# Attention heads on one core: scratch writes of GpSimd halved and partly left out, and a gather moved between two scatters

## The chip, the cores and the metric

One core of one Trainium2 chip. The metric is the device time of one execution in microseconds (us); the median of three runs of the kernel before is 1216.95 us (1214.2 to 1217.95).

## The reference, cut to what matters

A transformer layer: modulated layer norm, attention, then a mixture of experts. The change touches the attention alone. For each of 32 (batch, head) pairs the 409 queries of largest norm out of 2048 are picked; only they attend, and their results are put back at their places, zeros elsewhere.

```python
query_norms = jnp.linalg.norm(Q, axis=2)
_, top_idx = jax.lax.top_k(query_norms, top_u)          # 2048 // 5 = 409
Q_sel = jnp.take_along_axis(Q, top_idx[:, :, None], axis=1)
attn = jax.nn.softmax(jnp.einsum('bud,bld->bul', Q_sel, K) * scale, axis=-1)
out_sel = jnp.einsum('bul,bld->bud', attn, V)
out_full = out_full.at[jnp.arange(BH)[:, None], top_idx].set(out_sel)
```

## The kernel before, in words

The program is a row of blocks with a barrier between them: set-up, projection of Q, K and V, selection of the 409 queries, attention (`attend_block`, line 803, some 223 to 643 us), routing, experts. Only `attend_block` is touched.

It works through N = 32 heads in a software pipeline. Each head's 409 queries are three full chunks of 128 rows (FULL = 3) and a tail of 25 rows; the tails of four heads (GH = 4) share one tile, `qtail`. The engines' parts for head n:

- **TensorE** (`run`, line 1160): 16 score tiles of head n (`scores_tile`, line 1113, index j), and between them the 13 score chunks of the heads n + 1 and n + 2 (`scores_chunk`, lines 1097 and 1100), the transposes of the queries of head n + 3 (`turn_q`, lines 1068 and 1072, at j = 8, once per head), the products with V (line 1123), the folding of the result (line 1132) and the transposes of the row maxima (`turn_max`, line 1139, at j = 13). `turn_q` waits for the three gathers of its head and for the gather of the tails of its group of four.
- **VectorE** (line 961): one maximum over each of the 13 chunks (`maximum`, line 966), each raising the semaphore `a_done`; after a head's last one `minus_maximum` (lines 973 to 979): three small copies, a reduction, a cast to bfloat16 (line 978) and a subtraction, for which `turn_max` waits; and `finish` (lines 987 to 990) for the head before, which needs the scatters of two heads back to be over.
- **ScalarE** (line 1021): the exponentials (line 1036) and copies out of PSUM.
- **SyncE** (line 873): three loads of K per head.
- **GpSimd** (line 884): the irregular transfers. In its loop over n (line 937) it issues the three gathers of the queries of head n + 4 (`gather_chunk`, line 887), copies V of head n + 3 into its tile (`spread_v`, line 903), waits for `out_done`, and issues the three scatters of the results of head n - 1 (`scatter_chunk`, line 906). Every fourth head a gather of the tails of the next four heads (`gather_tails`, line 898) and a scatter of four heads' tails (`scatter_tails`, line 920) come after the three scatters.

What sets GpSimd's order is `turn(n, at)` (line 911), ahead of each of these transfers, seven times per head, also where no transfer follows. It writes a scratch tile `idle` of 128x512 float32 that nobody reads, waits for that write to end, and then waits until VectorE has done so many maxima: the thresholds are `13 (n + 1) + TURNS[at]` with TURNS = (7, 9, 11, 13, 15, 17, 19). So the three gathers wait for the maxima 7, 9 and 11 of head n + 1, the first scatter for its 13th and last, the next ones for the 2nd and the 4th of head n + 2, and the transfers of tails for the 6th.

Of the kernel before, what the change touches and what calls it, by code (L numbers as in the profile page):

```python
# [8 lines left out]

# [1 line left out]

# [3 lines left out]
F32 = mybir.dt.float32  # L17
# [8 lines left out]
P = 128  # L26
# [22 lines left out]
GH, GN = 4, N // 4  # L49
# [17 lines left out]
def wait(eng, sem, value):  # L67

    if isinstance(value, int) and value <= 0:
        return  # L70
    eng.wait_ge(sem, value)


def places(nc, own, block):

    sems = []

    def clear():
        nc.clear_and_free_semaphores(sems)
        nc.all_engine_barrier()  # L80

    def sem(name):
        sems.append(nc.alloc_semaphore(f"{block}_{name}"))
        return sems[-1]

    own.callback(clear)
    return (lambda name, shape, dt: own.enter_context(nc.sbuf_tensor(f"{block}_{name}", shape, dt)),
            lambda name, shape, dt: own.enter_context(nc.psum_tensor(f"{block}_{name}", shape, dt)),
            sem)
# [713 lines left out]
def attend_block(nc, ctx, io, cst):  # L803

    with ExitStack() as own:
        sb, ps, sem = places(nc, own, "attend")
        CH = 512
        NK = L // CH
        FULL = QT - 1
# [17 lines left out]
        recip = sb("recip", [P, QT], F32)  # L827
        outs, otail = cst["outs"], cst["otail"]
        fold = sb("fold", [P, HD + 1], F32)
        idle, idled = sb("idle", [P, 512], F32), sem("idled")  # L830
        p_a = [ps(f"p_a{i}", [P, 512], F32) for i in range(3)]
        p_b = [ps(f"p_b{i}", [P, 512], F32) for i in range(3)]
        p_o = ps("p_o", [P, 512], F32)
# [33 lines left out]
        def has(n):  # L867

            return not isinstance(n, int) or 0 <= n < N

        with nc.Block() as block:

            @block.sync
            def _(sp):
                def load_k(n, u):

                    wait(sp, b_ps, TPB * (n - U + 1))
                    rows = io["k3_d"][bass.ds(n, 1)].rearrange("a r d l -> (a r d) l")
                    for at, count in STACK_K:
                        sp.dma_start(kt[u][at * HD:(at + count) * HD, :], rows[0:count * HD, :]).then_inc(k_here[u], 16)  # L880

                steps(sp, load_k)

            @block.gpsimd
            def _(pool):
                def gather_chunk(n, c):
                    pool.indirect_dma_start(out=qsel[n % U][:, c, :], out_offset=None, in_=io["q3_d"],  # L887
                                            in_offset=bass.IndirectOffsetOnAxis(ap=cst["idx"][:, n, c:c + 1], axis=0)).then_inc(q_here[n % U], 16)

                def gather(n):  # L890
                    wait(pool, q_ps, n - U + 1)
                    for c in range(FULL):
                        gather_chunk(n, c)

                def gather_tails(g):

                    wait(pool, q_ps, GH * g)
                    pool.indirect_dma_start(out=qtail[:, :], out_offset=None, in_=io["q3_d"],
                                            in_offset=bass.IndirectOffsetOnAxis(ap=cst["tidx"][:, g:g + 1], axis=0)).then_inc(tail_here, 16)

                def spread_v(n):
                    wait(pool, pv_ps, GRP * (n - U + 1))
                    pool.tensor_copy(vh[n % U][:, :, 0:HD], vn[:, :, n, :]).then_inc(vh_done, 1)

                def scatter_chunk(n, c):
                    pool.indirect_dma_start(out=io["attn_d"], out_offset=bass.IndirectOffsetOnAxis(ap=cst["idx"][:, n, c:c + 1], axis=0),  # L906
                                            in_=outs[n % 2][:, c, :], in_offset=None).then_inc(scattered[n % 2], 16)

                TURNS = (7, 9, 11, 13, 15, 17, 19)

                def turn(n, at):

                    pool.memset(idle[:, :], 0.0).then_inc(idled, 1)  # L913
                    pool.wait_ge(idled, len(TURNS) * n + at + 1)
                    wait(pool, a_done, min(NA * (n + 1) + TURNS[at], NA * N))

                def scatter_tails(g):

                    pool.wait_ge(out_done, GH * (g + 1))
                    pool.indirect_dma_start(out=io["attn_d"], out_offset=bass.IndirectOffsetOnAxis(ap=cst["tidx"][:, g:g + 1], axis=0),  # L920
                                            in_=otail[:, g, :], in_offset=None).then_inc(tail_out, 16)

                gather_tails(0)
                for n in range(3):
                    gather(n)
                step = Chain(pool, g_step)
                step(pool.memset(fold[:, :], 0.0))
                for g in range(GRP):
                    last = pool.affine_select(out=fold[:, :], in_=fold[:, :], compare_op=ALU.not_equal, fill=1.0,
                                              base=-32 * g, pattern=[[-1, HD + 1]], channel_multiplier=1)  # L930
                    if g < GRP - 1:
                        step(last)
                last.then_inc(fold_done, 1)
                for n in range(3):
                    spread_v(n)
                gather(3)
                for n in range(N):
                    if has(n + 4):
                        pool.wait_ge(q_ps, n + 1)
                    for c in range(FULL):  # L940
                        turn(n, c)
                        if has(n + 4):
                            gather_chunk(n + 4, c)
                    if has(n + 3):
                        spread_v(n + 3)
                    if has(n - 1):
                        pool.wait_ge(out_done, n)
                    for c in range(FULL):
                        turn(n, FULL + c)
                        if has(n - 1):  # L950
                            scatter_chunk(n - 1, c)
                    turn(n, 2 * FULL)
                    if n % GH == 1 and n > 1:
                        scatter_tails(n // GH - 1)
                    if n % GH == 0 and n // GH + 1 < GN:
                        gather_tails(n // GH + 1)
                for u in range(2):
                    pool.wait_ge(scattered[u], 16 * FULL * (N // 2 - u))
                pool.wait_ge(tail_out, 16 * (GN - 1))
# [1015 lines left out]
```

## Time and profile before

| | |
|---|---|
| median of three runs | 1216.95 us |
| the profiled execution, its own time | 1216.12 us |
| its span in the trace | 1214.3 us |
| TensorE busy | 999.9 us, 82% of the span |
| VectorE busy | 906.4 us, 75% |
| ScalarE busy | 649.6 us, 53% |
| GpSimd busy | 740.3 us, 61% |
| GpSimd's scratch writes (line 913) | 224, 120.3 us |
| mean granted clock of TensorE | 0.90 of full speed |

The span is the trace's first to last instruction; the execution's own time has 1.8 us around it. Shares are means over all blocks: in the attention block alone they are others. An interval between two rows of the same line in neighbouring heads is the time that one head takes.

### The profile page before, as it was taken

Reading aid. Unit: us, or ns where it says so; the run is one execution under the profiler, and the core shown is the slowest. Engines: PE = TensorE matmul, PEld = TensorE weight load, DVE = VectorE, ACT = ScalarE, POOL = GpSimd, SP = SyncE. Lnnn points to the kernel's source line nnn. Section 1 sums busy time; section 2 is a strip of 40 time slices with the busy share of each in tenths; the row PEclk is TensorE's granted clock in tenths of the full one; section 3 lists DMA queues with packets and bytes.
Section 4 is the critical chain, followed back from the end, with each engine's and each line's share of the span. In section 5 each row is a group of like instructions: output and inputs, shape, how many; then the busy total and the mean of one; then the engine's idle time right before and its main releaser. Section 6 shows DMA issues by size and latency. Waiting matters only on the chain. (4 is left out here: it accounts for less than half of the span.)

```text
span 1214.3 us, 29465 instructions
## 1 busy us (share of the span) xinstructions
PE 999.9 (82%) x7725; PEld 613.1 (50%) x7726; DVE 906.4 (75%) x2189; ACT 649.6 (53%) x1448; POOL 740.3 (61%) x873
## 2 busy tenths in 40 slices
PE   7999101399999998999995774189999999999995
PEld 4444001133333332333334663167778888888894
DVE  3885689788887786887844887857778777777774
ACT  2777196067776775776773542344544444444441
POOL 1687382458888878888867884025445445544543
PEclk9999555579999998999997986589999999999998
DMA  6244772201111111111105993099893233222332
GB/s 225 104 143 162 242 234 67 59 18 47 35 46 32 45 33 32 46 45 33 32 4 182 268 280 103 5 251 226 218 222 62 47 50 52 43 47 48 52 44 27
DMA packets 129166, 118.71 MB, mean 98 GB/s; under 512 B 18064, under 2 KB 117072, under 8 KB 129104
## 3 DMA queue, kind: packets, MB, share of 16 engines
q1 hardware_dynamic: 106840, 95.02, 26.8%
q0 software_dynamic: 20480, 21.53, 11.1%
q10 hardware_dynamic: 1784, 1.44, 0.4%
q8 instruction: 26, 0.43, 0.2%
q14 instruction: 36, 0.29, 0.1%
HBM read 57.27 MB, written 37.60 MB: 78 GB/s over the span
## 5 line engine op out<-in xcount | busy, mean ns | idle before, releaser
L966 DVE TENSOR_REDUCE attend_mxh<-attend_p_a 128x1 f32<-128x512 f32 x416 | 265.2, 686 | 67.9 <-PE attend_p_a L1097 46.3
L1036 ACT ACTIVATE w<-attend_p_b 128x409 f32<-128x409 f32 x480 | 229.0, 514 | 107.8 <-PE attend_p_b L1113 90.0
L1730 POOL DMA_INDIRECT out_x<-expert_ys,expert_drop x72 | 122.0, 1695 | 193.2 <-DVE expert_ys L1872 138.5
L1837 ACT ACTIVATE expert_hr<-expert_p,b1t 128x256 f32<-128x256 f32 (+1 forms) x376 | 134.3, 424 | 195.6 <-PE expert_p L1775 132.2
L1113 PE MATMUL attend_p_b<-attend_qt,w 98*128 98x409 bf16 x480 | 165.7, 349 | 0.3 <-ACT w L1036 0.3
L1097 PE MATMUL attend_p_a<-w,attend_qt 96*128 96x512 bf16 x384 | 152.8, 401 | 3.3 <-ACT attend_qt L1027 1.9
L1797 PE MATMUL expert_p<-w,expert_hhi 128*128 x800 | 136.7, 273 | 0.6 <-DVE expert_ys L1872 0.2
L1775 PE MATMUL expert_p<-expert_xhi,w 128*128 128x256 f16 x800 | 136.4, 273 | 0.0
L913 POOL MEMSET attend_idle<- 128x512 f32 x224 | 120.3, 537 | 8.4 <-DVE otail L990 4.6
L1720 POOL DMA_INDIRECT expert_xs<-h_d,expert_take x72 | 74.0, 1027 | 74.7 <-DVE expert_take L1876 53.6
L1123 PE MATMUL attend_p_o<-w,attend_vh 128*32 128x409 f32 x1024 | 118.1, 534 | 1.1 <-ACT w L1036 0.6
L887 POOL DMA_INDIRECT attend_qsel<-q_d,idx x96 | 92.8, 966 | 38.2 <-POOL attend_idle L913 19.1
L906 POOL DMA_INDIRECT attn_d<-outs,idx x93 | 91.6, 985 | 30.7 <-DVE attend_mxh L966 16.1
L1797 PE MATMUL expert_p<-w,expert_hlo 128*128 x400 | 109.0, 273 | 0.0
L1113 PEld LDWEIGHTS attend_p_b<-attend_qt,w 98*128 98x128 bf16 x480 | 46.6, 98 | 115.7 <-ACT w L1036 78.2
L1897 DVE TENSOR_TENSOR expert_hlo<-expert_hr,expert_hhi 128x512 f16<-128x512 f32 x144 | 100.5, 698 | 5.0
L1895 DVE CAST expert_hhi<-expert_hr 128x512 f16<-128x512 f32 x144 | 62.8, 436 | 48.4 <-ACT expert_hr L1837 41.2
L1797 PEld LDWEIGHTS expert_p<-w,expert_hhi 128*128 128x128 f16 x800 | 78.2, 98 | 13.2 <-issue 3.7
L1775 PEld LDWEIGHTS expert_p<-expert_xhi,w 128*128 x800 | 78.3, 98 | 9.2
L1775 PE MATMUL expert_p<-expert_xlo,w 128*128 128x256 f16 x400 | 76.4, 273 | 0.0
L1775 PE MATMUL expert_p<-expert_xhi,expert_wu 128*128 128x128 f16 x704 | 67.2, 221 | 1.7 <-DVE expert_xlo L1880 1.4
L1792 PE MATMUL expert_p<-w,expert_hhi 128*128 x176 | 60.9, 380 | 5.3 <-DVE expert_ys L1872 2.8
(353 smaller groups left out, 1994.8 us busy)
## 6 DMA issues: line engine op xcount, KB each, us to landing
expert_wu<-w SPq DMA_DIRECT2D x88, 256.0 KB
q_d<-project_q SPq DMA_DIRECT2D x32, 256.0 KB
w<-in_L_ffn_w SPq DMA_DIRECT2D x16, 512.0 KB, 4.2
route_wraw<-in_L_ffn_w SPq DMA_DIRECT2D x16, 512.0 KB, 5.2
w<-k_d SPq DMA_DIRECT2D x32, 192.0 KB
k_d<-project_k SPq DMA_DIRECT2D x45, 128.0 KB
x<-in_L_attn_x SPq DMA_DIRECT2D x8, 512.0 KB, 8.8
attn_d<-zero SPq DMA_DIRECT2D x8, 512.0 KB
```

Of the source, the lines that this page charges most:

```text
L887: pool.indirect_dma_start(out=qsel[n % U][:, c, :], out_offset=None, in_=io["q3_d"], in_offset=bass.IndirectOffsetOnAxis(ap=cst["idx"][:, ...
L913: pool.memset(idle[:, :], 0.0).then_inc(idled, 1)
L966: dve.tensor_reduce(mxh[:, c, k:k + 1], chunk_bank(a)[:, :], AX, ALU.max).then_inc(a_done, 1)
L1036: act.activation(prob[:, j, :], tile_bank(j)[:, 0:TOP], ACT.Exp, scale=SCALE).then_inc(prob_done, 1)
L1097: last = pe.matmul(into[:, :], qt[u][0:KR, c * P:(c + 1) * P], kt[u][0:KR, k * CH:(k + 1) * CH], start=True, stop=True)
L1113: pe.matmul(tile_bank(j)[:, 0:TOP], kt[u][0:KR + 2, j * P:(j + 1) * P], qt[u][0:KR + 2, 0:TOP], start=True, stop=True).then_inc(b_ps, 1)
L1123: last = pe.matmul(p_o[32 * w:32 * w + VC, 0:TOP], vh[u][:, j, :], prob[:, j, :], start=(g == 0), stop=(g == TPB // GRP - 1), tile_positio ...
L1730: pool.indirect_dma_start(out=out, out_offset=bass.IndirectOffsetOnAxis(ap=drop[u][:, s:s + 1], axis=0), in_=ys[u][:, s, :], in_offset=Non ...
L1775: last = pe.matmul(p_1[g][:, f, rows], w, xp[u][:, k, rows], start=(n == 0), stop=(n == 3 * KD - 1))
L1797: last = pe.matmul(p_2[s][:, 0:D], hp[u][:, f, s * P:(s + 1) * P], w(slice(part, part + 1)), start=(f == 0 and n == 0), stop=(f == FB - 1 ...
L1837: last = act.activation(hr[g % 2][:, f, rows], p_1[g][:, f, rows], ACT.Relu, bias=cst["b1t"][:, bass.ds(e[s] * FB + 2 * g + f, 1)], scale= ...
L1897: dve.tensor_tensor(hlo[u][:, 2 * g:2 * g + 2, :], hr[g % 2][:, :, :], hhi[u][:, 2 * g:2 * g + 2, :], ALU.subtract).then_inc(hlo_done, 1)
```

## The change

GpSimd's part of `attend_block` alone. There are two scratch tiles of 128x256 elements in place of one of 128x512, used in turns, each with a semaphore of its own: a write waits for the write before the last one, and nothing waits for the write just issued. Ahead of the first scatter, behind the copy of V, nothing is written. Turns without a transfer behind them are left out. The gather of four heads' tails stands between the first and the second scatter (threshold 15), and in those heads the second and the third scatter wait for the thresholds 17 and 19.

```diff
-        idle, idled = sb("idle", [P, 512], F32), sem("idled")
+        idle, idled = [sb(f"idle{i}", [P, 256], F32) for i in range(2)], [sem(f"idled{i}") for i in range(2)]
...
+                rows = itertools.count()
+
+                def space():
+
+                    i = next(rows)
+                    wait(pool, idled[i % 2], i // 2)
+                    pool.memset(idle[i % 2][:, :], 0.0).then_inc(idled[i % 2], 1)
+
                 def turn(n, at):
 
-                    pool.memset(idle[:, :], 0.0).then_inc(idled, 1)
-                    pool.wait_ge(idled, len(TURNS) * n + at + 1)
+                    if at != FULL:
+                        space()
                     wait(pool, a_done, min(NA * (n + 1) + TURNS[at], NA * N))
...
                 for n in range(N):
                     if has(n + 4):
                         pool.wait_ge(q_ps, n + 1)
-                    for c in range(FULL):
-                        turn(n, c)
-                        if has(n + 4):
+                        for c in range(FULL):
+                            turn(n, c)
                             gather_chunk(n + 4, c)
                     if has(n + 3):
                         spread_v(n + 3)
+                    fresh = n % GH == 0 and n // GH + 1 < GN
+                    if fresh and not has(n - 1):
+                        turn(n, FULL + 1)
+                        gather_tails(n // GH + 1)
                     if has(n - 1):
                         pool.wait_ge(out_done, n)
-                    for c in range(FULL):
-                        turn(n, FULL + c)
-                        if has(n - 1):
+                        for c in range(FULL):
+                            turn(n, FULL + c + (fresh and c > 0))
                             scatter_chunk(n - 1, c)
-                    turn(n, 2 * FULL)
+                            if fresh and c == 0:
+                                turn(n, FULL + 1)
+                                gather_tails(n // GH + 1)
                     if n % GH == 1 and n > 1:
+                        turn(n, 2 * FULL)
                         scatter_tails(n // GH - 1)
-                    if n % GH == 0 and n // GH + 1 < GN:
-                        gather_tails(n // GH + 1)
```

## Rows read from the trace of the kernel before

**Rows 1.** Window: us; busy us (count) of PE, PEld, DVE, ACT, POOL; PE clock, DMA share, GB/s.

```profile
255.80:598.70 342.90, 335.75 (x2468) 120.69 (x2470) 277.71 (x614) 242.83 (x532) 287.19 (x402) 0.98 0.16 39
```

**Rows 2.** Timeline of TensorE, line 1068, once per head: start us, us, engine, line, operation.

```profile
255.76 0.35 PE L1068 MATMUL attend_p_a<-identb,attend_qsel 128*32 128x128 bf16 x9
...
267.39 0.35 PE L1068 MATMUL attend_p_a<-identb,attend_qsel 128*32 128x128 bf16 x9
...
302.44 0.35 PE L1068 MATMUL attend_p_a<-identb,attend_qsel 128*32 128x128 bf16 x9
...
314.58 0.35 PE L1068 MATMUL attend_p_a<-identb,attend_qsel 128*32 128x128 bf16 x9
...
448.76 0.35 PE L1068 MATMUL attend_p_a<-identb,attend_qsel 128*32 128x128 bf16 x9
...
463.56 0.51 PE L1068 MATMUL attend_p_a<-identb,attend_qsel 128*32 128x128 bf16 x9 [3.09 <-DMA attend_qtail<-q_d,tidx]
...
478.08 0.35 PE L1068 MATMUL attend_p_a<-identb,attend_qsel 128*32 128x128 bf16 x9
...
598.66 0.35 PE L1068 MATMUL attend_p_a<-identb,attend_qsel 128*32 128x128 bf16 x9
```

**Rows 3.** Waits, 242 to 640 us: who waits for whom, us in total, times, longest.

```profile
PE attend_p_a L1068 <- DMA attend_qtail<-q_d,tidx: 6.9, 4, 3.1
```

**Rows 4.** Timeline of GpSimd: one head and the next head's first gather.

```profile
337.68 1.00 POOL L887 DMA_INDIRECT attend_qsel<-q_d,idx  x1 [0.28 <-POOL attend_idle L913]
338.67 0.54 POOL L913 MEMSET attend_idle<- 128x512 f32 x1
...
343.38 1.02 POOL L906 DMA_INDIRECT attn_d<-outs,idx  x1 [0.28 <-DVE attend_mxh L966]
...
349.38 1.00 POOL L887 DMA_INDIRECT attend_qsel<-q_d,idx  x1 [0.28 <-POOL attend_idle L913]
```

**Rows 5.** Timeline of GpSimd where a gather of last rows comes between.

```profile
461.12 1.00 POOL L898 DMA_INDIRECT attend_qtail<-q_d,tidx  x1 [0.28 <-POOL attend_idle L913]
...
462.93 0.97 POOL L887 DMA_INDIRECT attend_qsel<-q_d,idx  x1 [0.27 <-POOL attend_idle L913]
```

**Rows 6.** Groups of GpSimd: count, busy us, mean ns of one, idle before it.

```profile
L913 POOL MEMSET attend_idle<- 128x512 f32 x224 | 120.3, 537 | 8.4 <-DVE otail L990 4.6 <-DVE attend_mxh L966 2.1
L887 POOL DMA_INDIRECT attend_qsel<-q_d,idx x96 | 92.8, 966 | 38.2 <-POOL attend_idle L913 19.1 <-DVE attend_mxh L966 13.2 <-issue 5.9
L906 POOL DMA_INDIRECT attn_d<-outs,idx x93 | 91.6, 985 | 30.7 <-DVE attend_mxh L966 16.1 <-POOL attend_idle L913 13.3 <-DMA attn_d<-outs,idx 1.4
...
L903 POOL COPY attend_vh<-v 128x256 f32<-128x256 f32 x32 | 12.8, 404 | 0.3
...
L1367 POOL MEMSET keepf<- 128x256 f32 x1 | 0.3, 318 | 0.0
```

**Rows 7.** Timeline of all engines around the cast of line 978, GpSimd late.

```profile
304.39 0.41 POOL L903 COPY attend_vh<-v 128x256 f32<-128x256 f32 x1
304.42 0.87 DVE L978 CAST attend_mpart<-attend_mneg 128x4 bf16<-128x4 f32 x1
...
304.73 0.53 POOL L913 MEMSET attend_idle<- 128x512 f32 x1
```

**Rows 8.** The same around a later cast, GpSimd on time.

```profile
599.21 0.69 DVE L966 TENSOR_REDUCE attend_mxh<-attend_p_a 128x1 f32<-128x512 f32 x1
...
600.63 0.17 DVE L978 CAST attend_mpart<-attend_mneg 128x4 bf16<-128x4 f32 x1
600.68 0.99 POOL L906 DMA_INDIRECT attn_d<-outs,idx  x1 [0.92 <-DVE attend_mxh L966]
```

**Rows 9.** The same around a cast that began under a gather's last 0.07 us.

```profile
426.22 0.97 POOL L887 DMA_INDIRECT attend_qsel<-q_d,idx  x1 [0.27 <-POOL attend_idle L913]
...
427.12 0.64 DVE L978 CAST attend_mpart<-attend_mneg 128x4 bf16<-128x4 f32 x1
427.18 0.55 POOL L913 MEMSET attend_idle<- 128x512 f32 x1
```

More of the change, by code:

```diff
@@ L12 @@
+import itertools
 from contextlib import ExitStack
```

## The prediction

> **What bounds the kernel now.** I read the attention block by stage first, then one row per head on TensorE, then who waits for whom, then GpSimd instruction by instruction. The window [rows 1] holds 28 heads: TensorE is busy in 335.75 of 342.90 us, GpSimd in 287.19. By busy share TensorE is the bound, and GpSimd has room. The other views correct that.
>
> TensorE turns each head's queries once, at a fixed place, so the distance between two such rows is the time of a head [rows 2]. Undisturbed it is 267.39 - 255.76 = 11.63 us, and that head has no gap on TensorE. The mean is (598.66 - 255.76) / 28 = 12.25 us. So 342.90 - 28 x 11.63 = 17.3 us are lost. A large part is lost at one kind of place: the turn of every fourth head, which waits for the gather of four heads' last rows (four such waits, 6.9 us [rows 3]). The worst is at 463.56, after 3.09 us of idleness. The two intervals around it last 14.80 and 14.52 us, 6.06 over twice 11.63: the matmul row itself is longer behind the idle stretch (0.51 against 0.35 us), which is the lower of the two clock levels, 1.2 instead of 2.4 GHz. The pattern comes four times in the 28 heads, and its eight intervals together have 14.8 us of the 17.3.
>
> Why that gather is late stands in GpSimd's timeline [rows 4]. From one head's first gather to the next one's pass 349.38 - 337.68 = 11.70 us without a pause that it chooses: a transfer of about 0.97, a write of 0.54, 0.27 to 0.28 until the next transfer. That is already over TensorE's 11.63. With a transfer of last rows it is 1.27 us more: 462.93 - 461.12 = 1.81 for transfer, write and gap [rows 5], less the 0.54 of a write that every head has there with nothing behind it. Per four heads, two of them with such a transfer, 4 x 11.70 + 2 x 1.27 = 49.3 us against TensorE's 46.5. **GpSimd is the bound**, though a quarter of its queue is scratch writes: 224 x 537 ns = 120.3 us [rows 6].
>
> The other 2.5 us of the 17.3 have another place. The cast of line 978 takes 0.17 us on its own [rows 8] and up to 0.87 where GpSimd works: begun at 304.42, 0.03 us behind GpSimd's copy, it ends at 305.29, 0.03 after the write that follows the copy [rows 7]. The transposes of the maxima wait for it. In that head the interval is 314.58 - 302.44 = 12.14, 0.51 over, so TensorE forgives about 0.87 - 0.51 = 0.36 us of cast.
>
> **The change, part by part.** The durations come from one execution, 1216.12 us with a span of 1214.3; the median of the runs is 0.8 above it.
>
> (a) Shorter scratch write. The nearest row is a GpSimd write of 128x256 float32 at 318 ns [rows 6], against 537.
>
> (b) Fewer of them. Three per head ahead of gathers in 28 heads, 84; two ahead of scatters in 31 heads, 62; seven ahead of each kind of last rows, 14: 160 for 224. The one ahead of the first scatter goes, and so does the empty turn in each head.
>
> (c) No wait for one's own write. What stands between a write and a transfer then? At best nothing (the gap passes under the write), at worst the time that a transfer needs when its semaphore comes late: the maximum that began at 599.21 ends at 599.90, the scatter it releases starts at 600.68, 0.78 us later [rows 8]. The write would then lie inside the 0.78. I take today's gap of 0.27, since most thresholds are long reached.
>
> GpSimd's sum for a plain head: 3 gathers x 0.966 + 3 scatters x 0.985 + copy 0.404 = 6.26 [rows 6]; 5 writes x 0.318 = 1.59; 6 gaps x 0.27 = 1.62; together 9.47 us. With last rows, 1.00 + 0.318 + 0.27 = 1.59 more: 11.06. Both are below 11.63, so GpSimd waits for VectorE at its thresholds instead of running behind, and cannot carry lateness into the next head.
>
> (d) The gather of last rows moves ahead of two scatters. It waits for the 2nd maximum instead of the 6th. Being issued on time, it ends some 4.2 us behind a head's last maximum: 0.73 to the cast [rows 8], 0.17 for it, about as much for the subtraction behind it, two maxima of 0.69, then 0.78 and 1.00. It lands 463.56 - 462.12 = 1.44 us later [rows 2, 5]. TensorE's row of line 1068 comes 599.90 - 598.66 = 1.24 us ahead of that maximum, so it wants the data 11.63 - 1.24 = 10.4 us behind it, over 4 us after they are there. Queued behind it are two scatters, delayed by at most 1.59 us; their reader is the result tile of two heads later, so that costs nothing while the cover of a whole head lasts. SyncE's queue is not passed. By these numbers the move matters little once (a) to (c) hold; were GpSimd late, it would bring the gather forward by two turns, about 3.1 us, as much as the longest wait.
>
> (e) The cast. With GpSimd on time it starts at 600.63 and the first scatter at 600.68: it keeps its 0.17 us. The pattern of rows 8 comes three times, at the last three casts, each time with the scatter 0.05 to 0.06 us behind the cast. That is inside the 0.36 that TensorE forgives. But whichever starts first goes first: in rows 7 and 9 GpSimd's work was there already or followed without a gap, and the cast waited; a timely scatter could do the same (rival 1).
>
> TensorE is late next, with every one of its 11.63 us filled; its granted clock is 0.98 of 2.4 GHz in the mean of the 28 heads with the four waits among them [rows 1], so I expect no new cost there. Sum: -14.8 - 2.5 = -17.3 us. In the block's end GpSimd's last scatter comes up to 1.8 us earlier, but VectorE's last result does not; I count 0 and keep -1.8 as an end of the range. 1216.12 - 17.3 = 1198.8 for the profiled execution, 1199.6 for the median.
>
> On this the Trainium skill, SBUF — State Buffer, Who interferes with whom, says that a VectorE copy or cast in its two-port mode and a GpSimd operation exclude each other, whichever starts first holding the ports to its end. The trace agrees (0.87 against 0.17). By that rule alone a scatter that wins the race costs a head what rival 1 says, and one that loses it costs nothing; which of the two it will be, the page cannot say.
>
> **The rivals.**
> 1. **The scatter beats the cast**, slower than before. The margin is 0.05 us (600.68 against 600.63). Nothing is written ahead of that scatter now; if that lets it start more than 0.05 earlier, the cast waits for it and for the write that follows without a gap. A cast that began 0.07 before a gather's end waited through the next write too, 0.64 [rows 9]. Price: 0.985 + 0.318 = 1.30 us of cast, less 0.36: 0.94 per head, 12.57 x 28 = 352.0, 9.1 over today's 342.9: 1226. Against it: the wait ahead of the scatter is the same semaphore after the same maximum. Chance 0.08.
> 2. **It beats it in half the heads.** 0.47 us per head, 13.2 of the 17.3 given back: 1213. Or with the cast held for the scatter alone, in some heads: around 1208. Chance 0.12.
> 3. **The gap is 0.78, not 0.27.** With the write inside it, a plain head takes 5.86 + 0.40 + 6 x 0.78 = 10.9 us and one with last rows 10.9 + 1.78 = 12.7; mean 11.8, over 11.63 again by 0.2: up to 28 x 0.2 = 5.6 given back: 1203 to 1205. Chance 0.07.
> 4. **Nothing changes**, because something else holds TensorE at 12.25. For it only the busy share of 98%; against it the undisturbed 11.63. 1217. Chance 0.05.
>
> **The numbers.** The forecast has 0.68 (1197.5 to 1202). The likeliest time is 1199.5. The range 1196 to 1211 takes in rival 3 and most of rival 2 and leaves out rivals 1 and 4, 0.13, and a part of 2. A measurement of this kernel can tell about 0.3%, 3.7 us, from no change. Faster by more than that: forecast, rival 3 and three quarters of rival 2, 0.84. Within it: the rest of 2 and rival 4, 0.08. Slower: rival 1, 0.08.
>
> **What would show it.** 160 writes near 318 ns; TensorE's row of line 1068 every 11.63 us, also at every fourth head, and no wait for the gather of last rows; GpSimd's idle time put down to VectorE's maxima, with a 0.78 us start after each; the cast at 0.17 in all heads. Wrong if casts of about 1 us appear, if GpSimd still goes from transfer to write to transfer without waits, or if intervals stay at 11.7 and more with GpSimd on time.

## The result, and the profile after

The changed kernel takes 1231.58 us (median of 4 runs, 1227.55 to 1236.65) against 1216.69 for the kernel before (4 runs): ratio 1.0139, interval 1.0112 to 1.0165. I had forecast 1199.5 and said "slower" with a chance of 0.08. The profiled execution took 1227.55 us with a span of 1225.7.

GpSimd's own part came nearly as computed. Its groups in the changed kernel (line, operation, names, count, then busy us, mean ns of one, idle before it and who ended it), to be held against [rows 6]:

```profile
L888 POOL DMA_INDIRECT attend_qsel<-q_d,idx x96 | 93.1, 970 | 59.8 <-DVE attend_mxh L978 49.9 <-issue 9.9
L907 POOL DMA_INDIRECT attn_d<-outs,idx x93 | 91.6, 984 | 87.8 <-DVE attend_mxh L978 76.9 <-issue 6.7 <-DVE otail L1002 3.8
...
L918 POOL MEMSET attend_idle<- 128x256 f32 x160 | 52.7, 329 | 0.2
```

160 writes of 329 ns take 52.7 us where 224 took 120.3, and the transfers now wait for VectorE's maxima instead of for GpSimd's own writes: GpSimd is on time. The groups of VectorE show the cast of line 990 at 173 ns in the mean, and no slow one among the 32:

```profile
L978 DVE TENSOR_REDUCE attend_mxh<-attend_p_a 128x1 f32<-128x512 f32 x416 | 267.3, 686 | 86.7 <-PE attend_p_a L1109 71.9 <-issue 9.3 <-PE attend_p_a L1112 0.2
...
L990 DVE CAST attend_mpart<-attend_mneg 128x4 bf16<-128x4 f32 x32 | 5.5, 173 | 1.1
```

No wait of TensorE for the four heads' last rows is left, where [rows 3] had 6.9 us. Undisturbed heads take 11.63 us, as forecast. But the window of the 28 heads is longer than before, not shorter (columns as in [rows 1]):

```profile
255.71:611.71 356.00, 343.64 (x2466) 121.01 (x2466) 272.12 (x614) 243.10 (x532) 231.56 (x352) 0.95 0.16 38
```

356.00 us, 13.1 over the 342.90 of [rows 1]. TensorE is busy in 343.64 of them, 7.9 more than before with the same matmuls, and idle in 12.4. Where the first loss comes from is to be seen in the timeline of all engines in the head whose turn is at 303.52, where the moved gather has just been issued and its two scatters follow (start us, us, engine, line, operation; weight loads and some rows left out):

```profile
309.05 1.00 POOL L907 DMA_INDIRECT attn_d<-outs,idx  x1 [0.17 <-issue]
...
310.04 0.34 POOL L918 MEMSET attend_idle<- 128x256 f32 x1
...
310.06 0.38 PE L1109 MATMUL attend_p_a<-w,attend_qt 96*128 96x512 bf16 x1
...
310.28 0.34 PE L1125 MATMUL attend_p_b<-attend_qt,w 98*128 98x409 bf16 x1
...
310.54 0.98 POOL L907 DMA_INDIRECT attn_d<-outs,idx  x1 [0.17 <-issue]
310.71 0.52 ACT L1048 ACTIVATE w<-attend_p_b 128x409 f32<-128x409 f32 x1
...
311.22 1.46 DVE L978 TENSOR_REDUCE attend_mxh<-attend_p_a 128x1 f32<-128x512 f32 x2 [1.54 <-PE attend_p_a L1109]
311.52 0.33 POOL L918 MEMSET attend_idle<- 128x256 f32 x1
...
311.95 0.91 ACT L1048 ACTIVATE w<-attend_p_b 128x409 f32<-128x409 f32 x2 [0.72 <-PE attend_p_b L1125]
```

TensorE's chunk of line 1109 that began at 310.06 ends at 310.44. VectorE, idle since 309.68, begins its maximum only at 311.22, 0.78 us later. The tile of line 1125 that began at 310.28 ends at 310.62; ScalarE is free at 311.23 and begins its exponential at 311.95. Both engines stand still though by these rows their input is computed. **What is late is the word that it is there**: the trace also has the times of the signals themselves (a signal is the update of a semaphore by which TensorE tells its reader), and it has a signal 0.02 to 0.1 us ahead of the reader's start in 17 of the 18 stops counted below, 0.5 to 1.7 us behind the end of the matmul's row, where the median over all tiles is 0.014. GpSimd meanwhile goes through a scatter, a write, a scatter and a write, begun 310.54 - 309.05 = 1.49 us apart. Eighteen such stops of ScalarE, of 0.5 to 1.8 us, lie in the 28 heads and add up to some 19 us (a stop is counted from 0.4 us between the later of the matmul's end and ScalarE's own, and the start of the exponential).

What follows a stop costs as much again. The windows of the head with that stop and of the next two (the third column from the end is the granted clock as a share of 2.4 GHz):

```profile
303.52:315.53 12.01, 11.81 (x89) 4.25 (x88) 8.97 (x22) 7.74 (x18) 9.12 (x15) 1.00 0.18 42
315.53:330.33 14.80, 13.35 (x89) 4.52 (x89) 10.57 (x24) 9.63 (x21) 9.53 (x15) 0.88 0.15 34
330.33:343.43 13.10, 13.10 (x89) 4.40 (x88) 9.88 (x24) 8.74 (x20) 7.74 (x13) 0.87 0.15 37
```

12.01, 14.80 and 13.10 us. In the second, TensorE is idle for 1.45 us and the granted clock falls to its lower level, 1.2 GHz, for a part of the head; the same 88 or 89 rows take 13.35 and 13.10 us of its time instead of 11.63. So the loss goes into idle time first and then into slower matmuls: of the 356.00 - 325.64 = 30.4 us over 28 heads of 11.63, 12.4 are idle time of TensorE and 18.0 are rows that take longer.

### The profile page after: what moved, and what is told of

Same layout as the page of the kernel before. It is cut to its first block and busy times, and to the rows that moved or that the text cites. A ratio compares the mean times of both kernels' runs of the same rounds, so it can differ in the third digit from the quotient of the medians.

```text
span 1225.7 us, 29249 instructions
## 1 busy us (share of the span) xinstructions
PE 1007.7 (82%) x7725; PEld 611.1 (50%) x7726; DVE 899.9 (73%) x2189; ACT 649.4 (53%) x1448; POOL 679.0 (55%) x809
## 3 DMA queue, kind: packets, MB, share of 16 engines
q10 hardware_dynamic: 1784, 1.44, 0.4%
## 5 line engine op out<-in xcount | busy, mean ns | idle before, releaser
L1125 PE MATMUL attend_p_b<-attend_qt,w 98*128 98x409 bf16 x480 | 168.6, 355 | 0.7 <-issue 0.5
L1135 PE MATMUL attend_p_o<-w,attend_vh 128*32 128x409 f32 x1024 | 122.7, 553 | 2.1 <-ACT w L1048 1.0
L553 PE MATMUL project_p_qv<-wtb,project_ht 128*128 128x512 f32 x128 | 60.0, 593 | 0.0
```

The lines of the kernel that those rows point to most:

```text
L1125: pe.matmul(tile_bank(j)[:, 0:TOP], kt[u][0:KR + 2, j * P:(j + 1) * P], qt[u][0:KR + 2, 0:TOP], start=True, stop=True).then_inc(b_ps, 1)
L1135: last = pe.matmul(p_o[32 * w:32 * w + VC, 0:TOP], vh[u][:, j, :], prob[:, j, :], start=(g == 0), stop=(g == TPB // GRP - 1), tile_positio ...
```

## Experiments

I started from the theory that GpSimd's transfers now follow one another too closely, with three rivals: that the missing wait for the own write does it by itself, that the moved gather does it, and that a GpSimd on time is in the way wherever it is. The first group of four had one ingredient taken out in each.

**e1_own_wait**, in `space()` of the changed kernel:

```diff
                     pool.memset(idle[i % 2][:, :], 0.0).then_inc(idled[i % 2], 1)
+                    pool.wait_ge(idled[i % 2], i // 2 + 1)
```

> The changed kernel, but every scratch write of 256 is waited for before the next transfer, as in the kernel before. In the changed kernel 19 or so stalls stand out, in which ScalarE and VectorE both sit idle though their inputs are there; each falls on the third (or fourth) GpSimd transfer in a row whose starts are 1.44 to 1.50 us apart. Crowding theory (what counts is the distance of the starts): the distance grows to 0.97 + 0.32 + 0.27 = 1.56 to 1.60 us; if the limit lies below that the time falls to about 1200 us, if above it, it stays within 8 us of the changed kernel's 1231. Own-wait theory (a write in flight under the preparation of the next transfer does the harm, the distance does not matter): the stalls vanish, 1198 to 1203 us.

Measured: 1196.08 us (4 runs), ratio 0.9839 (0.9807 to 0.9872). The 28 heads take 327.3 us, and 27 of them 11.63 to 11.69.

**e2_rows512**, the changed kernel with longer scratch rows:

```diff
-        idle, idled = [sb(f"idle{i}", [P, 256], F32) for i in range(2)], ...
+        idle, idled = [sb(f"idle{i}", [P, 512], F32) for i in range(2)], ...
```

> The changed kernel with the two scratch rows at 512 elements again, still in turns and without a wait for the own write. Crowding theory: the starts are 0.97 + 0.54 + 0.16 = 1.67 us apart, so fewer and shorter stalls or none, 1200 to 1215 us. Own-wait theory: the write is still in flight when the next transfer is prepared, so the stalls stay, 1225 to 1235 us.

Measured: 1194.92 us, 0.984 (0.9808 to 0.9873).

**e3_tails_back**, the changed kernel with the last rows gathered behind the scatters again:

```diff
-                            turn(n, FULL + c + (fresh and c > 0))
+                            turn(n, FULL + c)
                             scatter_chunk(n - 1, c)
-                            if fresh and c == 0:
-                                turn(n, FULL + 1)
-                                gather_tails(n // GH + 1)
...
+                    if fresh:
+                        turn(n, 2 * FULL)
+                        gather_tails(n // GH + 1)
```

> The changed kernel with the gather of four heads' last rows back behind the three scatters. Theory that the move alone does the harm (it makes rows of three and four close transfers out of pairs in seven heads): 1200 to 1210 us. Crowding theory in general: the last rows' transfer then stands before the next head's gathers and closes up with them, so the rows of three move but most of them stay: 1220 to 1232 us. Own-wait theory: no difference from the changed kernel, 1226 to 1236 us.

Measured: 1195.15 us, 0.9828 (0.979 to 0.9866), with 98 transfers begun under 1.52 us behind the one ahead of them, and no stop. No theory of mine had this time.

**e4_lean512**, the kernel before with its 512-element write and its wait, without the empty turns and without the write ahead of the first scatter:

```diff
-                    for c in range(FULL):
-                        turn(n, c)
-                        if has(n + 4):
+                        for c in range(FULL):
+                            turn(n, c)
                             gather_chunk(n + 4, c)
...
-                    turn(n, 2 * FULL)
...
+                    if at != FULL:
+                        pool.memset(idle[:, :], 0.0).then_inc(idled, 1)
```

> The kernel before with its one scratch row of 512 and its own wait, but without the empty turns and without the write ahead of the first scatter; the gather of last rows stays behind the scatters. GpSimd's sum is 3 x 0.966 + 3 x 0.985 + 0.404 + 5 x 0.537 + 6 x 0.27 = 10.6 us per plain head and 12.3 with last rows, mean 11.45, just below TensorE's 11.63. Crowding theory: starts stay 1.78 us or more apart and nothing stalls, so the heads run at 11.63 to 11.75 us: 1199 to 1206 us. If the timeliness of GpSimd itself is what hurts (its transfers on time collide with something), it is slow like the changed kernel, 1220 us or more.

Measured: 1199.71 us, 0.9866 (0.983 to 0.9902), 28 heads in 329.4 us.

Each ingredient alone seemed able to cure it, and e3 contradicted the crowding theory: the same pace as in the changed kernel, and nothing stopped. I read that as an interplay of all three, and looked for the place. That was a mistake: the group held no run of the changed kernel itself. The second group, on another occasion, tried the place.

**e5_wait_fresh** and **e6_wait_rest**: the wait of e1 only at the three writes ahead of the moved gather and the two scatters behind it (21 writes), and only at the other 139.

```diff
+                    if own:
+                        pool.wait_ge(idled[i % 2], i // 2 + 1)
...
-                        space()
+                        space(n % GH == 0 and n // GH + 1 < GN and at > FULL)
```

> The changed kernel, with GpSimd waiting for its own scratch write only at the three writes ahead of the moved gather and the two scatters behind it (one head in four, 21 writes of 160); everywhere else it goes on without that wait. Local theory: the trouble starts where the moved gather is followed without a pause by two scatters, and the later stalls of a group of four heads are its consequence. Then there are no stalls, 28 heads take 326 to 328 us, and the time is 1195 to 1198. Theory of the whole queue: the missing wait harms anywhere, and the moved gather only adds to it. Then most stalls stay, 28 heads take 345 us or more, and the time is 1215 to 1232.

> The complement of the run before: GpSimd waits for its own scratch write everywhere but at the three writes ahead of the moved gather and the two scatters behind it. Local theory: each group of four heads still has its first stall, in the head behind the moved gather, and loses at least 1 to 2 us there (7 x 1.5 = 10 us: 1205); if the later stalls are only its consequence they stay too, and the time is 1205 to 1230. Theory of the whole queue: with 139 of 160 waits back nearly nothing is left of the stalls, 1195 to 1199.

**e7_between_2_3**, with the gather one scatter later:

```diff
-                            turn(n, FULL + c + (fresh and c > 0))
+                            turn(n, FULL + c + (fresh and c > 1))
...
-                            if fresh and c == 0:
-                                turn(n, FULL + 1)
+                            if fresh and c == 1:
+                                turn(n, FULL + 2)
```

> The changed kernel, with the four heads' last rows gathered between the second and the third scatter instead of the first and the second. Order theory: a gather followed at 1.5 us by a scatter is what starts the stalls; one such pair is left per four heads, so stalls stay, 28 heads take 340 us or more, 1210 to 1232. Theory that two scatters must follow the gather closely: only one does, so stalls go, 326 to 328 us, 1195 to 1198. Theory that only the length of the close sequence counts: the sequence is as long as before, so stalls stay, though the same length gave none with the gather behind the scatters.

**e8_before_moved**, the kernel before with the move alone:

```diff
-                        turn(n, FULL + c)
+                        turn(n, FULL + c + (fresh and c > 0))
                         if has(n - 1):
                             scatter_chunk(n - 1, c)
+                        if fresh and c == 0:
+                            turn(n, FULL + 1)
+                            gather_tails(n // GH + 1)
```

> The kernel before with the move alone: scratch rows of 512 elements, the wait for each write and the empty turns stay, and the four heads' last rows are gathered between the first two scatters. My prediction's step on the move (with GpSimd late it brings the gather forward by two turns, about 3.1 us, as much as the longest wait): the waits for the last rows (6.9 us) and the slow heads around them go, 28 heads take 330 to 336 us instead of 342.9, 1204 to 1211; GpSimd's own total of 49.3 us per four heads stays over TensorE's 46.5, so not all is gained. Theory that the move by itself starts stalls: slower than before, 1220 to 1235. Theory that the move does nothing: 1215 to 1218.

Measured, beside 1214.94 for the kernel before: e5 1225.67 (1.0073, 1.0039 to 1.0107), e6 1205.84 (0.9926, 0.99 to 0.9952), e7 1229.81 (1.0116, 1.0084 to 1.0149), e8 1210.93 (0.9963, 0.9947 to 0.9978). The local theory fell: with the waits back at the moved gather the stops only come a transfer or two later (some 7 us behind the moved gather where it was some 4). What e5, e6 and e7 follow is the number of transfers begun under 1.52 us behind the one ahead of them, between 255 and 640 us: 67, 13 and 73, against 74 in the changed kernel and none in e8. e8 gains 4.0 us, less than I had expected: its 28 heads take 339.4 us, not 330 to 336, for the move clears only one of the four waits. The row of its waits has 5.8 us in three, against the 6.9 in four of [rows 3]:

```profile
PE attend_p_a L1071 <- DMA attend_qtail<-q_d,tidx: 5.8, 3, 3.2
```

The third group put the changed kernel beside e1 and e3, both unchanged, and a size between 256 and 512. **e9_after_again**, **e10_own_wait_again** and **e11_tails_back_again** have no new edit; **e12_rows384** is e2 with 384 for 512.

> The changed kernel once more, unchanged, beside two of the earlier variants, because the runs so far came in groups that shared no kernel but the one before: the changed kernel alone, then four variants that were fast, then three variants that were slow. Theory of the code: the stalls belong to what the kernel issues, so it is slow wherever it runs: 1226 to 1237, 28 heads 350 to 360 us. Theory of the place: whether the stalls come depends on the occasion or the place of a run, not only on the code; then it can come out at 1194 to 1200 here, or the two variants beside it come out at 1215 to 1235.

> The changed kernel with the wait for the own scratch write, as in the first group of runs (1196.08 there). Theory of the code: 1194 to 1198 again, all heads at 11.63 us. Theory of the place: if the changed kernel is slow beside it, this one is slow too, above 1205.

> The changed kernel with the last rows gathered behind the scatters again, as in the first group of runs (1195.15 there); it has the closest transfers of all that were fast (53 triples begun within 3.0 us), so it should show the influence of the place first. Theory of the code: 1192 to 1198 again. Theory of the place: if the changed kernel is slow beside it, this one comes out above 1215.

> The changed kernel with scratch rows of 384 elements instead of 256, still in turns of two and without an own wait: a write of about 0.43 us, transfers 1.5 to 1.6 us apart. Theory of the code, by spacing: it lies between 256 (1231) and 512 (1195); with transfers as far apart as in the variant with the own wait (1.53 us and more) it should be free of stalls, 1195 to 1199. Theory of the place: it goes with the changed kernel beside it, slow if that is slow.

Measured, beside 1215.49: e9 1221.15 (1.0059, 1.0035 to 1.0083), e10 1199.58 (0.9862, 0.983 to 0.9893), **e11 1225.92** (1.0095, 1.0057 to 1.0132), e12 1198.63 (0.9871, 0.9841 to 0.9902). The same e3 kernel that took 1195 is now as slow as the changed one: the interplay was none, and the occasion of a run counts. The two kernels whose transfers are 1.53 us and more apart (most of their close ones 1.56 to 1.60) stay fast. One of them has the own wait and the other has not, so it is the distance and not the wait. In e12's timeline of GpSimd the transfers follow at 320.49, 322.05 and 323.65:

```profile
320.49 0.97 POOL L929 DMA_INDIRECT attn_d<-otail,tidx  x1 [0.17 <-issue]
321.46 0.43 POOL L918 MEMSET attend_idle<- 128x384 f32 x1
322.05 1.00 POOL L888 DMA_INDIRECT attend_qsel<-q_d,idx  x1 [0.16 <-issue]
...
323.65 0.98 POOL L888 DMA_INDIRECT attend_qsel<-q_d,idx  x1 [0.17 <-issue]
```

and its window of 28 heads has 327.08 us, with the clock at its upper level throughout:

```profile
255.29:582.37 327.08, 326.72 (x2465) 119.14 (x2464) 269.44 (x615) 241.57 (x533) 248.27 (x353) 1.00 0.17 41
```

The fourth group had the changed kernel as a control (**e13_after_control**, no edit), e2 again (**e14_rows512_again**), and two questions: do the key loads take part, do the scratch rows?

```diff
 e15_keys_cut
-                        sp.dma_start(kt[u][at * HD:(at + count) * HD, :], rows[0:count * HD, :])...
+                        some = count * HD if isinstance(n, int) and n < U else 1
+                        sp.dma_start(kt[u][at * HD:at * HD + some, :], rows[0:some, :])...
 e16_no_rows
-                    if at != FULL:
-                        space()
                     wait(pool, a_done, min(NA * (n + 1) + TURNS[at], NA * N))
```

> The changed kernel unchanged, as the control of this group. If the stalls exist on this occasion: 1219 to 1237. If it comes out below 1202, this is an occasion without stalls, and the other three runs of the group tell nothing on their cause.

> The changed kernel with scratch rows of 512 elements and no own wait, so transfers 1.7 us apart, as in the first group (1194.92 there, on an occasion where nothing stalled). Pace theory: stalls need transfers begun 1.5 us apart or closer, so this one is free of the long ones wherever it runs: 1194 to 1200, beside a control above 1215. If spacing is not what counts, it is above 1210.

> The changed kernel with the key loads of all heads but the first ones cut to one row of each copy (3 rows for 96), so that most heads are computed with keys of earlier heads; everything else is as in the changed kernel. Theory that the key loads take part: without their bytes the stalls go, 28 heads take 326 to 330 us, 1194 to 1200. Pace theory in its plain form (GpSimd's transfers alone): the stalls stay, 1219 to 1237.

> The changed kernel without any scratch write: transfers follow one another as soon as their thresholds allow, some 1.25 us apart where they are late and 1.4 us and more where VectorE's maxima hold them. Pace theory: at least as many stalls as in the changed kernel, 1219 to 1245. Theory that the scratch rows themselves are at fault (the signals are let go when a write ends): no writes, no stalls, 1194 to 1202, and the casts stay at 0.17 us.

Measured, beside 1216.08: **e13 1193.56** (0.9829, 0.9788 to 0.9869), e14 1194.56 (0.9821), e15 1193.18 (0.9822), e16 1195.54 (0.9829). The very kernel that took 1231.6 and 1221.2 takes 1193.6 here, and nothing stops in any of the four, so e14 to e16 tell nothing on the cause. In e15 most heads are computed with the keys of earlier heads, and its results are wrong; only its time is used. The window of its 28 heads, against 356.00 above:

```profile
251.90:577.60 325.70, 325.70 (x2468) 119.22 (x2469) 269.44 (x615) 242.36 (x533) 231.95 (x353) 1.00 0.17 41
```

325.70 us, TensorE busy in all of it. The place in its timeline that answers to the stop shown above, with GpSimd's two scatters 1.50 apart (303.93, 305.43):

```profile
303.93 0.99 POOL L907 DMA_INDIRECT attn_d<-outs,idx  x1 [0.17 <-issue]
...
304.95 0.38 PE L1109 MATMUL attend_p_a<-w,attend_qt 96*128 96x512 bf16 x1
...
305.17 0.34 PE L1125 MATMUL attend_p_b<-attend_qt,w 98*128 98x409 bf16 x1
...
305.37 1.29 DVE L978 TENSOR_REDUCE attend_mxh<-attend_p_a 128x1 f32<-128x512 f32 x2 [0.81 <-PE attend_p_a L1109]
305.43 0.97 POOL L907 DMA_INDIRECT attn_d<-outs,idx  x1 [0.17 <-issue]
305.61 0.92 ACT L1048 ACTIVATE w<-attend_p_b 128x409 f32<-128x409 f32 x2
```

The chunk begun at 304.95 ends at 305.33, the maximum begins at 305.37: 0.04 us, against 0.78.

**A mark of the occasion.** Looking for what tells the traces apart, I found it ahead of the first head, in code that the change does not touch and that the kernel before has too: GpSimd gathers the first three heads' queries, nine transfers 1.25 us apart, while TensorE turns the first head's queries and ScalarE copies them. The timeline there, of the kernel before:

```profile
232.47 0.94 POOL L887 DMA_INDIRECT attend_qsel<-q_d,idx  x1 [0.30 <-issue]
...
233.38 0.20 PE L1072 MATMUL attend_p_a<-identb,attend_qtail 25*32 25x25 bf16 x3
233.72 0.95 POOL L887 DMA_INDIRECT attend_qsel<-q_d,idx  x1 [0.30 <-issue]
234.89 0.51 ACT L1027 ACTIVATE attend_qt<-attend_p_a 96x409 bf16<-96x409 f32 x1 [21.14 <-PE attend_p_a L1072]
234.97 0.95 POOL L887 DMA_INDIRECT attend_qsel<-q_d,idx  x1 [0.30 <-issue]
```

and of e13:

```profile
231.25 0.94 POOL L888 DMA_INDIRECT attend_qsel<-q_d,idx  x1 [0.30 <-issue]
...
231.95 0.20 PE L1084 MATMUL attend_p_a<-identb,attend_qtail 25*32 25x25 bf16 x3
...
232.20 0.51 ACT L1039 ACTIVATE attend_qt<-attend_p_a 96x409 bf16<-96x409 f32 x1 [19.63 <-PE attend_p_a L1084]
232.50 0.94 POOL L888 DMA_INDIRECT attend_qsel<-q_d,idx  x1 [0.30 <-issue]
```

In e13 ScalarE copies 232.20 - 232.15 = 0.05 us behind TensorE's last turn. In the kernel before it begins 234.89 - 233.58 = 1.31 us behind it, though it has been idle for 21 us. Over the 20 traces this delay is 0.05 in all eight of the first and the fourth group, and 1.3 to 2.2 in the other twelve, the first two kernels among them. It parts the occasions without one exception, whether the kernel then stops in its heads or not. The same twelve traces also lack a part of the signals' records: some 395 to 445 of the 512 of TensorE's tile signals in the block are there, and 507 or more in the other eight; e8, e10 and e12, which have no long stop, lack them too, so it is not a consequence of long stops. Where the records are missing says more. In the first 222 us, where GpSimd issues no transfer, both kinds of trace have as many (2773 to 2835 records of all semaphores, and 2771 to 2835). From 223 to 242 us, with the gathers 1.25 us apart, the twelve have 180 to 203 and the eight 401 to 433. So neither the late copy nor the missing records are seen before GpSimd's indirect transfers begin.

With the mark the last two runs could be read whatever the occasion: **e17_keys_cut_again** and **e18_no_rows_again** are e15 and e16 unchanged.

> As e15_keys_cut: the changed kernel with the key loads of all heads but the first ones cut to one row of each copy. If the trace again has all signals of line 1125 it is an occasion without stalls, 1190 to 1197, and tells nothing new. If a fifth of them is missing: with the key loads as a part of the cause 1190 to 1200 all the same; with GpSimd's transfers alone as the cause 1219 to 1237.

> As e16_no_rows: the changed kernel without any scratch write. On an occasion without stalls 1192 to 1199 and nothing new. On one with them: by pace, with transfers 1.25 us apart where they are late, 1219 to 1245; if the scratch rows are at fault, 1192 to 1202.

Measured, beside 1214.23, with the mark at 1.85 and 2.17 us: e17 1230.54 (1.0103, 1.0046 to 1.016), e18 1224.29 (1.0076, 1.0047 to 1.0105). The mark had been found after the fact, in the first 18 traces; these two fit it. Neither the bytes of the key loads nor the scratch rows are needed for the stops; the key loads were still issued in e17, with one row each, so that they take no part at all isn't shown. In e18 89 transfers begin under 1.52 us behind the one ahead, nearly all of them 1.25 to 1.3, and 40 stops of ScalarE lie in its heads. One of them, under two gathers 1.27 us apart and no write:

```profile
299.47 0.96 POOL L888 DMA_INDIRECT attend_qsel<-q_d,idx  x1 [0.30 <-issue]
...
300.74 0.95 POOL L888 DMA_INDIRECT attend_qsel<-q_d,idx  x1 [0.30 <-issue]
...
301.10 0.35 PE L1123 MATMUL attend_p_b<-attend_qt,w 98*128 98x409 bf16 x1
...
302.61 0.51 ACT L1046 ACTIVATE w<-attend_p_b 128x409 f32<-128x409 f32 x1 [1.09 <-PE attend_p_b L1123]
```

The tile begun at 301.10 ends at 301.45, its exponential begins at 302.61.

All runs in one table. "Close" counts the transfers that begin under 1.52 us behind the one ahead, 255 to 640 us; the last column is the delay of ScalarE's first copy.

| run | us | ratio | close | 28 heads, us | mark, us |
|---|---|---|---|---|---|
| before | 1216.7 | 1 | 0 | 342.9 | 1.31 |
| after | 1231.6 | 1.014 | 74 | 356.0 | 2.20 |
| e5 | 1225.7 | 1.007 | 67 | 358.0 | 1.95 |
| e6 | 1205.8 | 0.993 | 13 | 333.2 | 1.86 |
| e7 | 1229.8 | 1.012 | 73 | 361.4 | 1.51 |
| e8 | 1210.9 | 0.996 | 0 | 339.4 | 1.73 |
| e9 (after) | 1221.2 | 1.006 | 80 | 348.2 | 1.89 |
| e10 (as e1) | 1199.6 | 0.986 | 0 | 327.0 | 1.91 |
| e11 (as e3) | 1225.9 | 1.010 | 73 | 357.7 | 1.91 |
| e12 | 1198.6 | 0.987 | 0 | 327.1 | 1.72 |
| e17 | 1230.5 | 1.010 | 72 | 361.0 | 1.85 |
| e18 | 1224.3 | 1.008 | 89 | 357.8 | 2.17 |
| e1 | 1196.1 | 0.984 | 0 | 327.3 | 0.05 |
| e2 / e14 | 1194.9 / 1194.6 | 0.984 / 0.982 | 0 / 0 | 325.7 / 327.3 | 0.05 |
| e3 | 1195.2 | 0.983 | 98 | 327.3 | 0.05 |
| e4 | 1199.7 | 0.987 | 0 | 329.4 | 0.05 |
| e13 (after) | 1193.6 | 0.983 | 98 | 325.7 | 0.05 |
| e15 | 1193.2 | 0.982 | 98 | 325.7 | 0.05 |
| e16 | 1195.5 | 0.983 | 100 | 329.1 | 0.05 |

For long stops both are needed: an occasion with the mark, and transfers that keep beginning 1.5 us or less apart. All four combinations are in the table: with the mark and close, 1221 to 1232 us (e6, with 13 close ones alone, 1206); with the mark and not close, 1199 and 1200 (e10, e12); without the mark 1193 to 1200, close or not. Above 67 close transfers their number no longer orders the times (80 go with 348.2 us, 67 with 358.0). A few traces lack rows of transfers as well, so the counts of the upper part are low by some.

## Why the prediction was wrong, and where it was right

**(a), (b), the shorter and fewer writes**: right, 160 writes at 329 ns where I took 318. (In the kernel before they were no quarter of GpSimd's time, as I wrote, but 7 x 0.537 = 3.76 of a head's 11.70 us, nearly a third; the sums don't use the quarter.)

**(c), no wait for one's own write**: this is the step that failed. I priced the gap on GpSimd alone, "at best nothing", at worst the 0.78 us of a late semaphore, and took 0.27. The gap is 0.17 us, better than that. But the wait did two things, and I counted one: it also kept the transfers apart. With 329 ns and 0.17 they begin 1.44 to 1.50 us apart, and on an occasion with the mark TensorE's signals then come late to ScalarE and VectorE. With the wait and the same 256 elements the distance is 1.53 and more, and on such an occasion the time is 1199.6 us (e10; e1's 1196.1 comes from one where nothing stops anyway). The difference of some 0.1 us per transfer (medians of the close ones 1.47 and 1.58) is worth 22 to 26 us there, by e9 and e11 beside e10. All my bounds for this step were GpSimd's own time; none was for what a denser GpSimd does to others. The mechanism was in none of my rivals.

**The sentence on TensorE**, "every one of its 11.63 us filled; ... so I expect no new cost there", failed with it. It holds word for word in e13 (325.70 busy of 325.70) and not in the changed kernel's first trace (343.64 of 356.00, the clock 0.95 in the mean). The last of my signs of being wrong, intervals of 11.7 and more with GpSimd on time, is what came.

**(d), the move**: costs nothing that shows, as said; e11 without it and e9 with it both stop, e3 without and e13 with it do not. On the late GpSimd of the kernel before it was to bring the gather forward by two turns and clear the waits; it cleared one of four (e8).

**(e), the cast**: right in the kernels with 256 elements and no own wait, 0.173 us in the mean; rivals 1 and 2 did not occur. With the own wait it is 0.20 to 0.22, with 512 elements 0.24 to 0.26: in some heads a write meets it again (up to 0.62 in e2). That a cast in its two-port mode and a GpSimd operation exclude each other, the first to start holding the ports to its end, is what the Trainium skill says in SBUF — State Buffer, Who interferes with whom; by that rule too a cast that starts ahead of the scatter keeps its 0.17 us. The trace agrees: in the changed kernel none of the 32 casts begins under a GpSimd operation, and the next one follows 0.05 us behind it at the closest.

**Rival 3** (the gap of 0.78) did not occur: a semaphore that was reached long ago costs 0.16 to 0.17, only one that comes late costs more. **Rival 4** did not occur either.

**The sum.** 342.9 - 17.3 = 325.6 us for the 28 heads; e13 has 325.70. So on an occasion without the mark the forecast stands for the 28 heads. I had counted nothing outside them, and there e13's trace is shorter too: its span is 24.2 us below the kernel before's, of which 17.2 lie in the 28 heads, 3.9 ahead of them (they begin at 251.9, not 255.8) and 3.1 behind them. So even this run, 1193.6 us, falls below the stated 1196. And it does not save the forecast: the kernel that it was compared with was measured on an occasion with the mark, and so were most groups of runs here, three of five after it.

What the trace of before could have told: ScalarE's first copy, 1.31 us late under gathers 1.25 us apart. I read the block's heads and not its start, which the change leaves alone. It was the place in that trace where GpSimd works at the pace that the change brings to the heads, and even closer, and there a reader of TensorE's results was late without a reason of its own.

**What stays open**: what an occasion with the mark is. It isn't told by the number of the chip in the results, since the first group (no mark) and the second (marked) bear the same one. Every execution here was taken by the profiler, and those with the mark are those that lost records, so it isn't shown either that the recording has no part in the delays. And the signal's own time is late, but the rows can't say whether it is held up itself or the write into PSUM ahead of it is: the end of a matmul's row is modelled. The Trainium skill, Perfetto Trace Analysis, Tensor Engine Instruction, says that the profiler estimates this end and that the semaphore goes out when PSUM has acknowledged all bytes; by that both are possible, and no run here parts them. Nor is there more on the threshold than that 1.44 to 1.50 us are too close and that 1.56 to 1.60, where most of e10's and e12's close transfers lie (the closest 1.53), are not; a finer series of sizes was not tried.

**A version that beats both**: the changed kernel with the own wait (e1, e10) or with 384 elements (e12): ratios 0.984, 0.986 and 0.987, on occasions of either kind for the first, on a marked one for the second.

## What to carry to other kernels

A spacing operation can have a second use that its own cost doesn't show: before one is shortened or its wait dropped, look for the stretch of the trace where the engine already runs at the new pace, and see how late the readers of the other engines' results are there. Keep some margin from the pace at which readers come late, for going closer brought nothing that can be told here (without the mark, 325.7 and 327.3 us for the 28 heads with transfers mostly 1.68 us apart, 325.7 to 327.3 with 1.47) and cost 22 to 27 us where it went wrong. And put the kernel under study into every group of runs: a variant that is fast on another occasion proves nothing, and I built a theory on one.

## What the runs showed of the hardware

- Under GpSimd's indirect transfers begun 1.25 to 1.50 us apart, ScalarE and VectorE begin 0.4 to 2.9 us late on results of TensorE on some occasions, and not at all on others. At 1.53 us and more there are only shorter delays, of ScalarE alone: 13 of 0.6 to 0.8 us in the 28 heads of e10 and 7 of 0.5 to 0.8 in e12, which cost nothing to 0.26 us of a head; at 1.76 us and more 2 to 4 of 0.4 to 0.6 (the kernel before, e8).
- The same program, run on three occasions: 1231.6, 1221.2 and 1193.6 us, each within 0.8% in itself, while the medians of the kernel before stayed within 1214.2 and 1216.7 on all six.
- On those occasions a part of the semaphores' records is missing from the trace, from GpSimd's first indirect transfer on and not before: 180 to 203 records in 223 to 242 us against 401 to 433 on the others.
- The wait for a write that has just ended leaves 0.27 to 0.28 us to the next transfer [rows 4], no wait for it 0.17; 128x256 float32 takes 0.33 us to write, 128x384 0.43 to 0.44, 128x512 0.54.
